# Two-layer transformer kernel on one core: layer 1's constants loaded during layer 0, fewer unread wide matmuls, and gelu's table loaded ahead

## The reference

```
layer 0 attention: 32 query heads, 8 key/value heads of 64, RMS norm of q and k, rotary positions,
                   causal with a window of 64 keys, output projection 2048 -> 256
layer 0 ffn:       silu(gate(xn)) * up(xn), then down; 704 hidden; int32 weights less 128, with scales
layer 1 attention: second layernorm with weights, 16 heads of 16, rotary on half of each head,
                   full softmax over 1024 keys, output projection, plus its own input
layer 1 ffn:       weights = xn @ W_r + b_r, one number a token
                   the 64 tokens of each batch with the largest weights go through
                   gelu(x W1 + b1) W2 + b2 (1024 hidden), times their weight;
                   the tokens above the 64th weight are replaced by that, the others keep x
```

## Time and profile before

| | us |
|---|---|
| median of 3 runs | 1067.54 |
| lowest, highest | 1065.38, 1068.62 |
| the profiled execution | 1060.71 |
| its span | 1058.1 |
| PE busy | 1008.4 |
| DVE busy | 889.7 |
| ACT busy | 798.7 |
| POOL busy | 707.5 |

### The profile page before, as it was taken

How to read it: one execution, slowest core, us unless ns; L and a number is a source line. 1 busy time by engine, 2 the same in 40 slices (tenths; PEclk the granted TensorE clock), 3 DMA queues, 4 the chain that set the end, 5 groups by cost and what they waited for, 6 DMA issues and landing times. The chain is left out here.

```text
span 1058.1 us, 27432 instructions
## 1 busy us (share of the span) xinstructions
PE 1008.4 (95%) x8903; PEld 647.2 (61%) x8903; DVE 889.7 (84%) x1926; ACT 798.7 (75%) x2120; POOL 707.5 (67%) x984
## 2 busy tenths in 40 slices
PE   4899999999999999999999998999999999999997
PEld 2678888878878788788888874443333333333233
DVE  7988888888888988898898886689989889888872
ACT  4766777777777777777777773279999999888984
POOL 6898789889888888888797783314556463443320
PEclk9999999999999999999999999999999999999999
DMA  8111010010000000000001000500000000000001
GB/s 281 45 51 32 19 27 25 16 29 24 23 21 23 25 22 23 23 21 24 24 13 25 19 19 12 178 1 8 2 2 2 2 3 2 12 12 17 7 2 41
DMA packets 45951, 30.56 MB, mean 29 GB/s; under 512 B 27572, under 2 KB 43892, under 8 KB 45556
## 3 DMA queue, kind: packets, MB, share of 16 engines
q1 hardware_dynamic: 45156, 28.59, 9.3%
q10 hardware_dynamic: 656, 0.24, 0.1%
HBM read 18.36 MB, written 4.19 MB: 21 GB/s over the span
## 5 line engine op out<-in xcount | busy, mean ns | idle before, releaser
L1388 DVE TENSOR_REDUCE l_mxv<-l_mx 128x1 f32<-128x1024 f32 x256 | 300.6, 1219 | 40.3 <-PE l_mx L1633 37.7
L1263 ACT ACTIVATE l_prob<-l_sc 128x512 f32<-128x512 f32 x512 | 271.2, 609 | 18.3 <-PE l_sc L1641 16.5
L750 POOL TENSOR_TENSOR rm<-ss,half_neg 128x5 f32<-128x5 f32 x128 | 160.3, 1252 | 7.9 <-DVE ss L658 7.9
L1633 PE MATMUL l_mx<-l_kt,l_qt 48*128 48x512 f16 x512 | 154.1, 381 | 8.2 <-DVE l_mxv L1388 7.6
L759 POOL TENSOR_TENSOR t<-t 128x320 f32<-128x320 f32 x128 | 111.1, 868 | 74.9 <-DVE t L625 73.6
L1641 PE MATMUL l_sc<-l_qt,l_kt 50*128 50x512 f16 x512 | 159.2, 382 | 0.4 <-ACT l_prob L1263 0.3
L1614 PE MATMUL l_acc<-l_prob,qkv_all 128*17 128x256 f32 x2048 | 153.9, 384 | 0.0
L917 PEld LDWEIGHTS pv<-v,probs 128*128 128x128 f32 x1024 | 130.6, 191 | 10.4 <-issue 5.0
L917 PE MATMUL pv<-v,probs 128*128 128x65 f32 x1024 | 130.0, 270 | 0.9 <-ACT probs L506 0.9
L392 ACT ACTIVATE nat<-t 128x256 f16<-128x256 f32 (+1 forms) x256 | 79.2, 361 | 63.0 <-POOL t L777 61.9
L506 ACT ACTIVATE probs<-sc,neg_bound 128x512 f32<-128x512 f32 x128 | 88.0, 687 | 23.1 <-PE sc L947 19.9
(11 more groups left out here) (241 smaller groups left out, 2513.0 us busy)
## 6 DMA issues: line engine op xcount, KB each, us to landing
v<-v SPq DMA_DIRECT2D x240, 16.2 KB, 1.8
qkv_all<-w_qkv SPq DMA_DIRECT2D x3, 768.0 KB, 8.5
xn_all<-xs SPq DMA_DIRECT2D x16, 128.5 KB, 2.0
xa<-x SPq DMA_DIRECT2D x16, 128.0 KB, 2.4
qkv_all<-w_o SPq DMA_DIRECT2D x4, 512.0 KB, 5.1
xc<-x SPq DMA_DIRECT2D x16, 128.0 KB, 2.3
out<-xc SPq DMA_DIRECT2D x16, 128.0 KB, 1.9
l_wt<-w SPq DMA_DIRECT2D x2, 1024.0 KB, 5.6
```

What stands on the lines that cost most here:

```text
L750: return pool.tensor_tensor(dst, src, half_neg[:, 0:k], ALU.pow)
L1263: act.activation(prob[:, (y * NI + u) % NPR, h * 512:(h + 1) * 512], sc[:, k % NSC, :], ACT.Exp, scale=D1 ** -0.5).then_inc(s_["act_sc"], 1)
L1388: dve.tensor_reduce(mxv[:, x % 2, u:u + 1], mx[:, MX[k] % 2, :], AX.X, ALU.max).then_inc(s_["dve_mx"], 1)
L1633: ins = pe.matmul(mx[:, MX[kx] % 2, keys], qt[r:r + KS, tile % 4, u * P:(u + 1) * P], kt[r:r + KS, tile % 4, keys], start=True, stop=True)
```

## The change

Four things. (1) `brt`, `bef` and `iot` move out of layer 1: `brt` is loaded with layer 1's weights at s = 16 of layer 0, `before` at s = 40 into the buffer that held the masks, `slots` at s = 124 into the first half of the buffer that held the norm weights; layer 1's waits for them go. Buffers are shared for it (`rest` also serves as `thr_r`, a part of `sums` as `pos`). (2) The unread matmuls: 12 become 5 behind the threshold's transpose, 3 become 2 behind each of the six groups of transposes with c < 5, and `KEEP_AT` has 2 for 5 at (5, 0), and new entries of 5 at (5, 3) and 2 at (6, 3). (3) ScalarE issues a gelu of one column at (5, 3), whose result is overwritten. (4) ScalarE makes the high parts of the split of c = 1, and POOL only its low parts. The diff, without the signatures and declarations that only hand buffers on:

```diff
@@ layer0, buffers
-        nw = sb("nw", [P, 2, HD])
+        nw = nw_iot
...
-        mk = sb("mk", [P, 2, P], F16)
+        mk = mask_bef[:, :].bitcast(F16).rearrange("p (j t) -> p j t", j=2)
@@ layer0, SP, fetch
                     sp.dma_start(wr[:, :], w_r.broadcast_to([P, D])).then_inc(l1w_ld, 16)
+                    sp.dma_start(brt[:, :], b_r.broadcast_to([P, 1])).then_inc(l1w_ld, 16)
+                if s == 5 * G:
+                    sp.wait_ge(s_["pe_S"], B * G)
+                    sp.wait_ge(s_["set_mk"], 2)
+                    sp.dma_start(mask_bef[:, :], before).then_inc(mk_ld, 16)
+                if s == NT * G - 4:
+                    sp.wait_ge(s_["pool_tcw"], NI * 4)
+                    sp.dma_start(nw_iot[:, 0, :], slots.broadcast_to([P, CAP])).then_inc(nw_ld, 16)
...
+            sp.wait_ge(mk_ld, 16 * 2)
+            sp.wait_ge(nw_ld, 16 * 2)
@@ layer0, ScalarE and VectorE
-                    act.wait_ge(l1w_ld, 16 * 4)
+                    act.wait_ge(l1w_ld, 16 * 5)
...
-                        dve.wait_ge(l1w_ld, 16 * 4)
+                        dve.wait_ge(l1w_ld, 16 * 5)
@@
-KEEP_AT = {(5, 0): 5, (5, 1): 2, (5, 2): 2, (5, 7): 2, (6, 2): 2, (6, 5): 2}
+KEEP_AT = {(5, 0): 2, (5, 1): 2, (5, 2): 2, (5, 3): 5, (5, 7): 2, (6, 2): 2, (6, 3): 2, (6, 5): 2}
@@ layer1, buffers
-        bef = sb("bef", [P, P])
+        bef = mask_bef
-        iot = sb("iot", [P, CAP])
+        iot = nw_iot[:, 0, :]
-        thr_r = sb("thr_r", [B, P])
+        thr_r = rest[:, 1, 0:P]
-        pos = sb("pos", [P, B, NI])
+        pos = sums[:, 2, :, NI:]
@@ layer1, SP
-            sp.dma_start(brt[:, :], b_r.broadcast_to([P, 1])).then_inc(ld_br, 16)
-            sp.dma_start(bef[:, :], before).then_inc(ld_s, 16)
-            sp.dma_start(iot[:, :], slots.broadcast_to([P, CAP])).then_inc(ld_s, 16)
-            sp.wait_ge(ld_s, 16 * 2)
@@ layer1, ScalarE
+                if (c, u) == GATHER_AT[0]:
+                    act.activation(hid[:, 0, 0:1], idf[:, 0:1], ACT.Gelu_apprx_tanh)
...
+            q, k, q_hi, k_hi, q_lo, k_lo = parts_of(1)
+            ev(q_hi, q.unsqueeze(2).broadcast_to([P, NI, 2, D1]))
+            ev(k_hi, k.unsqueeze(2).broadcast_to([P, NI, 2, D1])).then_inc(s_["act_hi"], 1)
             for c in range(SLOTS):
@@ layer1, VectorE
             split(0)
-            dve.wait_ge(ld_br, 16)
...
-            dve.wait_ge(ld_s, 16 * 2)
@@ layer1, POOL
-                    pool.tensor_copy(q_hi, q.unsqueeze(2).broadcast_to([P, NI, 2, D1]))
-                    pool.tensor_copy(k_hi, k.unsqueeze(2).broadcast_to([P, NI, 2, D1])).then_inc(s_["pool_hi"], 1)
-                    pool.wait_ge(s_["pool_hi"], c - min(1, c // 2))
+                    if c > 1:
+                        pool.tensor_copy(q_hi, q.unsqueeze(2).broadcast_to([P, NI, 2, D1]))
+                        pool.tensor_copy(k_hi, k.unsqueeze(2).broadcast_to([P, NI, 2, D1])).then_inc(s_["pool_hi"], 1)
+                        pool.wait_ge(s_["pool_hi"], c - 1 - min(1, c // 2))
+                    else:
+                        pool.wait_ge(s_["act_hi"], 1)
@@ layer1, PE
-            keep_running(12)
+            keep_running(5)
...
-            pe.wait_ge(ld_s, 16 * 2)
...
                         if c < LAG_X:
-                            keep_running(3)
+                            keep_running(2)
```

More of the change, by code:

```diff
@@ L81, in build @@
         ranked = ctx.enter_context(nc.sbuf_tensor("ranked", [B, 2, CAP + P], F32))
+        rest = ctx.enter_context(nc.sbuf_tensor("rest", [B, 2, CAP + P], F32))
+        mask_bef = ctx.enter_context(nc.sbuf_tensor("mask_bef", [P, P], F32))
+        nw_iot = ctx.enter_context(nc.sbuf_tensor("nw_iot", [P, 2, HD], F32))
+        brt = ctx.enter_context(nc.sbuf_tensor("brt", [P, 1], F32))
         xn2_all = ctx.enter_context(nc.sbuf_tensor("xn2_all", [P, NT, D + 1], F32))
         qkv1_all = ctx.enter_context(nc.sbuf_tensor("qkv1_all", [P, ITEMS * NI * (2 * D1 + VW)], F32))
-        layer0(nc, ctx, idf, idh, ranked, xn2_all, qkv1_all, x, w_qkv, w_o, qk_w, w_gate, w_up, s_gu, w_down, s_down,
-               ln_w, ln_b, w_in, w_r, b_r, pos_table, masks, eye, out)
-        layer1(nc, idf, idh, ranked, xn2_all, qkv1_all, w_out1, b_r, w1, b1, w2, b2, before, slots, out)
+        layer0(nc, ctx, idf, idh, ranked, rest, mask_bef, nw_iot, brt, xn2_all, qkv1_all, x, w_qkv, w_o, qk_w, w_gate, w_up, s_gu, w_down, s_down,
+               ln_w, ln_b, w_in, w_r, b_r, pos_table, masks, eye, before, slots, out)
+        layer1(nc, idf, idh, ranked, rest, mask_bef, nw_iot, brt, xn2_all, qkv1_all, w_out1, w1, b1, w2, b2, out)
 def chunk(f):
@@ L163, in wait, with layer0 @@
         eng.wait_ge(sem, count)
-def layer0(nc, whole, idf, idh, ranked, xn2_all, qkv1_all, x, w_qkv, w_o, qk_w, w_gate, w_up, s_gu, w_down, s_down,
-           ln_w, ln_b, w_in, w_r, b_r, pos_table, masks, eye, out):
+def layer0(nc, whole, idf, idh, ranked, rest, mask_bef, nw_iot, brt, xn2_all, qkv1_all, x, w_qkv, w_o, qk_w, w_gate, w_up, s_gu, w_down, s_down,
+           ln_w, ln_b, w_in, w_r, b_r, pos_table, masks, eye, before, slots, out):
     with ExitStack() as ctx:
@@ L1074, in max_units, with layer1 @@
     return {unit: k for k, unit in enumerate(order)}
-def layer1(nc, idf, idh, ranked, xn2_all, qkv1_all, w_out1, b_r, w1, b1, w2, b2, before, slots, out):
+def layer1(nc, idf, idh, ranked, rest, mask_bef, nw_iot, brt, xn2_all, qkv1_all, w_out1, w1, b1, w2, b2, out):
     SC = score_units()
@@ L1160, in layer1 @@
         sch = [sc[:, j, :].bitcast(F16) for j in range(NSC)]
-        ld_s, ld_w, ld_w1, ld_w2, ld_x1, ld_br = (sem(n) for n in "ld_s ld_w ld_w1 ld_w2 ld_x1 ld_br".split())
+        ld_w, ld_w1, ld_w2, ld_x1 = (sem(n) for n in "ld_w ld_w1 ld_w2 ld_x1".split())
         MOD = {n: k + 1 for order in ("thrt pos spr0 spr1 xg xgt hid0 hid1 blk",
@@ L1169, in layer1 @@
                  "pe_sc act_sc pe_mx dve_mx pe_pv act_acc "
-                 "pe_ct dve_ct act_ct dve_ctx pe_y dve_y set_acc pool_xf pool_base dve_split").split()
+                 "pe_ct dve_ct act_ct dve_ctx pe_y dve_y act_hi set_acc pool_xf pool_base dve_split").split()
         s_ = {n: sem(n) for n in names}
@@ L1342, in _ @@
             split(2)
-            dve.wait_ge(ld_s, 16 * 2)
             dve.wait_ge(s_["mod_dve"], MOD["off"])
             dve.wait_ge(s_["mod_pe"], MOD["pos"])
-            dve.tensor_tensor(pos[:, :, :], acc[:, 0:B * NI].rearrange("p (b i) -> p b i", b=B), off[:, :, :],
+            dve.tensor_tensor(pos, acc[:, 0:B * NI].rearrange("p (b i) -> p b i", b=B), off[:, :, :],
                               ALU.add).then_inc(s_["mod_dve"], 1)
@@ L1349, in _ @@
             dve.tensor_tensor(hot[:, :, :, :].rearrange("p i b c -> p b i c"),
[L1350 to L1351 removed]
+                              iot.unsqueeze(1).unsqueeze(1).broadcast_to([P, B, NI, CAP]),
+                              pos.unsqueeze(3).broadcast_to([P, B, NI, CAP]),
                               ALU.is_equal).then_inc(s_["mod_dve"], 1)
@@ L1525, in _ @@
             pe.wait_ge(s_["mod_dve"], MOD["thr"])
-            pe.transpose(acc[:, 0:B], thr_r[:, :], idf[0:B, 0:B]).then_inc(s_["mod_pe"], 1)
-            keep_running(12)
+            pe.transpose(acc[:, 0:B], thr_r, idf[0:B, 0:B]).then_inc(s_["mod_pe"], 1)
+            keep_running(5)
             ranks = acc[:, 0:B * NI].rearrange("p (b i) -> p b i", b=B)
-            pe.wait_ge(ld_s, 16 * 2)
             pe.wait_ge(s_["mod_dve"], MOD["sum3"])
```

6 lines of the change are left out of this document (1 added, 5 removed).

## The result

| | before | after |
|---|---|---|
| median | 1061.26 (13 runs) | 1056.51 (13 runs) |
| lowest, highest | 1059.77, 1068.62 | 1054.72, 1059.74 |
| the profiled execution | 1060.71 | 1056.24 |
| its span | 1058.1 | 1054.4 |

The account below looks back on a forecast made before the run. PE, busy 95% of the span, was taken as the bound, with unread matmuls on its chain. 2.8 + 0.65 + 0.7 = 4.15 us, so 1067.54 - 4.15 = 1063.4; own range 1061.3 to 1065.3, 8 in 10 1060.6 to 1066.8.

Parts of the forecast that it names:

- The boundary: Begin of layer 1: fewer unread matmuls bring the first maxima 2.8 us earlier, 2.4 if the clock stays high.
- the second case: Begin of layer 1 at the high clock: five unread matmuls end at 662.6 and PE waits until 663.5; gain 2.4 us.
- The layer 0 loads: Three constant loads moved from layer 1 into layer 0: cost there taken as 0, bounds 0 and 0.5 us.
- KEEP_AT (5, 0): Slot 5, start: five unread matmuls become two, taking 0.65 us off the path.
- (5, 3): Slot 5, where PE idles 1.12 us for DVE: five unread matmuls added, costing 0, at most 0.1 us.
- The table: Gelu's table load of 1.28 us moved into ScalarE's idle time: hidden layer's second half 0.7 us earlier.
- Rival B: The table load stays in front of the gelu, so 0.7 us are missing: 1064.1; chance 0.06.
- ScalarE's high parts: Begin of layer 1: ScalarE instead of POOL makes the high parts of c = 1; worth 0 on the path.
- The sum: Whole kernel: 2.8 + 0.65 + 0.7 = 4.15 us gained, bounds 3.6 and 4.5.
- A: Around layer 1's begin: a second low-clock stretch from fewer wide matmuls, costing 1.75 us; time 1065.1, chance 0.14.
- D: Slower: the clock falls again between 668 and 690, where PE has gaps; time 1071, chance 0.04.
- C: The stretch gains but later waits, such as DVE late in slot 7, take it back; time 1067, chance 0.09.

Follow-up runs that it names:

- undo_act_high: The changed kernel with POOL making the high parts of c = 1 again; median 1056.75 us, ratio 0.9944.
- no_slot_keeps: The changed kernel with an empty KEEP_AT, the early gelu and the unread matmuls ahead of slot 5 staying; median 1060.96 us, ratio 0.9985.
- no_boundary_keeps: The changed kernel with none of the unread matmuls ahead of slot 5 (4, 5 and six times 2 removed); median 1056.73 us, ratio 0.9952.
- only_keeps: The kernel before with all the new counts of unread matmuls and nothing else; median 1058.96 us, ratio 0.9971.

## Why the prediction was wrong, and what of it was right

**The boundary**, 2.8 us, or 2.4 if the clock stays high there. Right at the high clock: 2.2 to 2.6 (10.06 and 10.44 for 7.88). The 2.8, with the low stretch in both kernels, no trace shows; the 3.2 against the first trace compares twelve in the low stretch with five outside it. "PE does not idle" was worked out for five matmuls at 1.2 GHz; at 2.4 PE idles 1.02 us, where the second case has 0.9. By the prediction's own list, a wait for DVE of over 0.3 us was a sign that it is wrong; the list overlooked that case. The ranks came at 663.30 for the 663.6 forecast, the first maxima at 667.79 for 668.6. DVE's sums were ready at 663.25 for the 663.4 worked out.

**The layer 0 loads**, 0. Right as far as the traces tell: layer 1's first matmul came between 659.53 and 660.35 in six kernels with the loads moved (659.91 in after), and between 659.77 and 660.52 in the five without. In two more (undo_act_high and no_slot_keeps) it came at 661.53 and 661.17, and both have a low stretch at 630.

**KEEP_AT (5, 0)**, 0.65: measured 0.65 (1.85 to 1.20). **(5, 3)**, 0 to 0.1: measured 0.00. **The table**, 0.7: measured 0.69 in the traces of before and after (5.40 to 4.71). That the two added at (6, 3) would take back 0.58 us of the load's 1.28 was right in kind; it was 0.44 of 1.13. Rival B is out.

**ScalarE's high parts**, 0 on the path. Perhaps mis-sized by 0.3 us, by one trace (undo_act_high). I had costed the casts for who waits for them, and DVE's sums at the one duration of the earlier trace rows; they are now what PE waits for, and they were 0.37 us longer in the one trace without this part, for a cause that is open.

**The sum**, 4.15: the profiled executions lie 4.47 apart (by the partly cancelling differences given above), the medians of the shorter runs 4.26 (1060.77 and 1056.51). What remains of the difference in medians, 4.75, and in the ratio, 5.6, is the long runs of before.

**The base.** The step that failed is this sentence: "The median of the runs shown lies 6.8 above it; nothing in the change touches what makes that distance, so 1067.54 - 4.15 = 1063.4". The step took the median of three runs as the kernel's usual time, and a distance of 6.8 us as fixed. What the runs showed in its place: before's median over 13 runs is 1061.26, 0.55 above the profiled execution, because only about a fifth of its runs are long, with more time at 1.2 GHz, and all three shown were such. Of the miss of 6.9 us, 6.3 are this (1067.54 less 1061.26), and 0.6 is the rest (4.75 for 4.15), part of it that the change takes the long runs away. So the second half of the sentence failed as well: the one long run that was traced has its low stretches behind the two gaps of the earlier trace rows, and the change closes both. That all three runs shown were long ones was bad luck (0.21 cubed is 1%), if they were drawn like the others, which the record can't show, but a profiled execution 4.7 us below the lowest of them said that two kinds of run exist, and that should have been asked: which of the two will be left? A sum against 1060.71 would have given 1056.6.

**The rivals.** A, a second low stretch: not beside the first one but instead of it; the trace of after has one stretch at the boundary or behind, as before, only at 699.5. It came where PE waits for ScalarE in slot 7, and cost 1.3 us. Of the rule that I had weighed for A (the Trainium skill, TensorE: Matmul & The Clock Gate, Part 4: PE-mode transpose) this much can be said: with pairs of wide matmuls between the six groups of transposes the granted clock was 1.00 from 663.3 to 668 in after; with none between them (no_boundary_keeps) it was 0.51 from 660 to 667, but there PE had also been idle for 2.78 us, so that the rule itself is neither shown nor refuted. D, gaps that let the clock fall between 668 and 690: the mechanism and its place were right, and I priced it as a danger of the changed kernel, though "PE has gaps of 1.12 and 1.06 us there already" was in the text. A danger that stands in the trace of before belongs to before. C, taken back later: only these 1.3 us. The Trainium skill, TensorE: Matmul & The Clock Gate, What's actually happening, says that the clock's monitor runs free of the kernel; the traces agree: with the same code before, the stretch near the boundary lay at 661.5 in one execution and at 679 in the other.

**Open.** There is one trace of a long run of before. That the others also spent more time at 1.2 GHz is on record, but that they did so behind the same gaps is inferred. Why a stretch falls in slot 7 in one execution and at 630 or 1047 in others (both in undo_act_high) wasn't found. The moved loads were not run by themselves; their 1.0 us is the difference of only_keeps and undo_act_high, 1.3 if the longer sums of the latter are an accident of its trace.

## What to carry to other kernels

Before an edit's gain is set against a median, compare the profiled execution with every run shown: a distance much larger than the spread is a second kind of execution, and if its cause may lie in the stretch being edited, the sum goes against both. If each run's granted clock is at hand, look at it first: here it told the long runs apart (0.990 or lower in 19 of 22, in none of the 92 shorter ones). Price unread matmuls one gap at a time: those that stood in a real wait were free (0.00 us), and those that stood where PE had work cost their full length (1.3 us of the six, 0.44 of the two). But judge what they do for the clock by the spread of the runs and not by the median alone: without the boundary's, the median stayed and five of twelve runs were 5 to 9 us above the fastest. When the engine that bounded a stretch is relieved, its successor's small instructions (DVE's sums here) are worth a bound of their own, since a difference like the 0.37 us seen in one trace now reaches the path.

## What was not expected of the hardware

Two gaps of 1.12 and 1.05 us, 15 us apart, had low stretches of 3.4 and 10.2 us behind them in one execution of before (beginning 1.7 and 0.3 us after PE went on), and none in another; in 21% of 127 runs the time was 3 to 9 us above the others. DVE's comparison and three adds of 128x16 took 1.06 to 1.12 us in thirteen traces and 1.44 in one, for no cause that I could show. And in the trace of no_boundary_keeps 7 us at 1.2 GHz with short real work only brought the first maxima 1.3 us earlier than the unread matmuls that prevent them, though other runs of that kernel paid for it.
